# Third and fourth layer norms moved by batches into the experts' loop and the mixer's steps, with the near experts gated and added in one instruction

## The reference, cut to what matters

```
x = x + attention(norm(x))     # 16 heads, top-32 scores of each row, three mixing rounds
x = x + experts(norm(x))       # route each token to one of 8 experts, capacity T/8
x = x + mixer(norm(x))         # conv, chunked state space scan, inner norm, projection
x = x + experts(norm(x))       # the same experts again

norm(x)    = (x - mean) / sqrt(var + 1e-5)
experts(x): logits = x @ wg; one expert a token, a position in it by a running count;
            y = gate * (x @ W[expert].T + b[expert]), gate 0 where the expert is full
mixer(u):   z, xBC, dt = u @ W_in.T; dt = softplus(dt + bias); ...
```

## Time and profile before

| | us |
|---|---|
| median of three runs (lowest, highest) | 2993.7 (2985.3, 3005.35) |
| the profiled execution, as timed | 2987.16 |
| its span in the profile | 2985.5 |
| busy in the span: DVE, PE | 2681.5 (90%), 2536.5 (85%) |
| busy in the span: POOL, ACT | 2258.9 (76%), 2064.4 (69%) |

### The profile page before, as it was taken

How to read it: one execution, slowest core, us unless ns; L and a number is a source line. 1 busy time by engine, 2 the same in 40 slices (tenths; PEclk the granted TensorE clock), 3 DMA queues, 4 the chain that set the end, 5 groups by cost and what they waited for, 6 DMA issues and landing times. The chain is left out here.

```text
span 2985.5 us, 56906 instructions
## 1 busy us (share of the span) xinstructions
PE 2536.5 (85%) x16480; PEld 1487.4 (50%) x16480; DVE 2681.5 (90%) x6598; ACT 2064.4 (69%) x6275; POOL 2258.9 (76%) x2816
## 2 busy tenths in 40 slices
PE   5788888888888888888888888888888787998857
PEld 3444444444444444444444444454444435777733
DVE  7999999999999999999999999999999374766646
ACT  3788888888888888888888888888887242222214
POOL 4899999999999999998998999999989251222105
PEclk7899999999999999999999999999999796767769
DMA  4444444444444444444444444444443000000001
GB/s 122 119 123 118 120 117 121 124 119 124 119 119 117 121 121 120 121 121 120 117 120 117 122 120 124 120 124 118 123 114 106 12 23 15 8 8 0 1 12 47
DMA packets 373454, 286.18 MB, mean 96 GB/s; under 512 B 30174, under 2 KB 369192, under 8 KB 373160
## 3 DMA queue, kind: packets, MB, share of 16 engines
q1 hardware_dynamic: 372232, 280.62, 33.1%
q10 hardware_dynamic: 928, 2.10, 0.2%
HBM read 139.48 MB, written 136.58 MB: 92 GB/s over the span
## 5 line engine op out<-in xcount | busy, mean ns | idle before, releaser
L1038 DVE MAX8 top<-work 128x8 f32<-128x512 f32 x1536 | 1012.5, 723 | 0.0
L1047 DVE MATCH_REPLACE8 work<-top,work 128x512 f32<-128x512 f32 x1024 | 707.1, 720 | 0.0
L1124 POOL TENSOR_TENSOR scores<-scores,cut 128x512 f32<-128x512 f32 x512 | 642.1, 1276 | 0.0
L657 PE MATMUL bank<-probs_t,u 128*64 128x512 f32 x2048 | 475.0, 606 | 11.5 <-ACT u L893 1.4
L1116 POOL TENSOR_SCALAR cut<-scores,minus_max_and_least 128x512 f32<-128x512 f32 x512 | 355.8, 695 | 46.9
L945 ACT ACTIVATE probs_of_tile<-scores,minus_max_and_least 128x512 f32<-128x512 f32 x512 | 376.3, 767 | 14.6 <-POOL scores L1124 14.6
L1137 POOL TENSOR_SCALAR probs_of_tile<-probs_of_tile,inverse 128x512 f32<-128x512 f32 x512 | 350.8, 696 | 26.9 <-DVE inverse L1004 1.4
L1047 DVE MATCH_REPLACE8 work<-top,scores 128x512 f32<-128x512 f32 x512 | 353.2, 719 | 0.0
L1035 DVE MAX8 top<-scores 128x8 f32<-128x512 f32 x512 | 336.5, 721 | 7.8 <-ACT scores L886 6.7
L1120 POOL TENSOR_SCALAR cut<-cut 128x512 f32<-128x512 f32 x512 | 306.6, 615 | 21.6
L864 ACT ACTIVATE band<-band 128x129 f32<-128x129 f32 x512 | 155.2, 305 | 225.6 <-DMA band<-probs_scratch 225.3
(11 more groups left out here) (272 smaller groups left out, 5080.5 us busy)
## 6 DMA issues: line engine op xcount, KB each, us to landing
probs_scratch<-probs_of_tile SPq DMA_DIRECT2D x256, 256.0 KB, 2.4
band<-probs_scratch SPq DMA_DIRECT2D x256, 256.0 KB, 3.2
rel_scratch<-rel SPq DMA_DIRECT2D x256, 254.0 KB, 3.1
relj<-rel_scratch SPq DMA_DIRECT2D x256, 128.0 KB, 2.3
relj<-rel_scratch SPq DMA_DIRECT2D x512, 64.0 KB, 2.5
experts_xs<-stream_normed_t SPq DMA_DIRECT2D x16, 256.0 KB, 2.3
stream<-in_L_attn_a_x SPq DMA_DIRECT2D x4, 512.0 KB, 8.4
mixer_xs<-stream_normed_t SPq DMA_DIRECT2D x8, 256.0 KB, 2.4
```

The costliest lines, as they stand in the source:

```text
L657: last = nc.tensor.matmul(U[HEADS[h], lo:hi], lhs, pt[mpar][:, h, jt, lo:hi], start=(jt == 0 and lo == 0), stop=(jt == NT - 1 and step > 0))
L1038: nc.vector.max(top[q][:, h, 8 * rnd:8 * rnd + 8], work[:, h, :]).then_inc(s.next_tops, 1)
L1047: nc.vector.match_replace(out=work[:, h, :], in_to_replace=top[q][:, h, 8 * rnd:8 * rnd + 8], in_values=sc[Tc][:, h, :] if rnd == 0 else w ...
L1124: nc.gpsimd.tensor_tensor(sc[Tc][:, h, :], sc[Tc][:, h, :], cut[:, h, :], ALU.add).then_inc(s.masked, 1)
```

## The change

The two `norm` blocks, their buffers and helpers, and `eight_tensor` are removed. The third norm is done group by group inside the loop of experts1, the fourth inside the mixer's steps:

- DVE: `group_merge`, four `bn_stats` and four `bn_aggr`, once POOL has added a group into the stream (experts1, after tile 2 of the next group) or after the batch's last `into_stream` (mixer).
- POOL: `group_shift`, two small instructions (variance + eps, minus the mean), the power, and one product that gives the shift.
- ACT: `group_spread`, four `Identity` activations with scale and bias per row, in place of the DVE scaling. It stands at the end of ACT's work on the following group (experts1) or of the step (mixer).
- PE: `group_turn` (four transposes), ACT: `group_keep` (the copy to `XNT`), PE: `group_products` (four tiles of 8 columns). In experts1 the transposes of group i-2 come behind the gate transposes of group i. In the mixer they go into bank `PX` ahead of the projections, which from batch 3 on wait for ACT's copy; the products go into the spare columns of `T1` at the end of the step, ACT copies them out, and from batch 3 on the next step's first write to `T1` waits for that copy (`logits_kept`). The mixer gets one step more.

In both experts, the loads `xs` and `gs` are gone: PE reads `XNT` and the gates in place. The buffer `near` is gone: for each tile DVE issues four `scalar_tensor_tensor` (near bank times gate, plus far) that write `sums`, after ACT's far gating; the near bank is now free only after them. The gate transposes and the bias have one bank each instead of two. All loops over groups and steps are written out instead of run by a loop. The output goes out in eight DMAs of 256 KB, each once its group is done. Last, at the start of the attention, POOL's eight additions of the output bias wait until DVE has scaled all groups, where each waited for its own.

```diff
+def group_merge(nc, dve, s, w, X, i):
+    for c in range(4):
+        last = nc.vector.bn_stats(w.stats[:, i, c, :], X[:, (i * 4 + c) * D:(i * 4 + c + 1) * D])
+    last.then_inc(s.stats, 1)
+    dve.wait_ge(s.stats, i + 1)
+    for c in range(4):
+        last = nc.vector.bn_aggr(w.mv[:, i, c, :], w.stats[:, i, c, :])
+    last.then_inc(s.merged, 1)
+
+def group_shift(nc, pool, s, w, i):
+    pool.wait_ge(s.merged, i + 1)
+    nc.gpsimd.tensor_scalar(w.vareps[:, i, :], w.mv[:, i, :, 1], EPS, 1.0, ALU.add, ALU.mult).then_inc(s.parts, 1)
+    nc.gpsimd.tensor_scalar(w.minus[:, i, :], w.mv[:, i, :, 0], -1.0, 0.0, ALU.mult, ALU.add).then_inc(s.parts, 1)
+    pool.wait_ge(s.parts, 2 * i + 2)
+    nc.gpsimd.tensor_tensor(w.rstd[:, i, :], w.vareps[:, i, :], w.mhalf[:, :], ALU.pow).then_inc(s.rstd, 1)
+    pool.wait_ge(s.rstd, i + 1)
+    nc.gpsimd.tensor_tensor(w.shift[:, i, :], w.minus[:, i, :], w.rstd[:, i, :], ALU.mult).then_inc(s.shift, 1)
+
+def group_spread(nc, act, s, w, X, i, xn):
+    act.wait_ge(s.shift, i + 1)
+    for c in range(4):
+        last = nc.scalar.activation(xn[:, c * D:(c + 1) * D], X[:, (i * 4 + c) * D:(i * 4 + c + 1) * D], ACT.Identity,
+                                    scale=w.rstd[:, i, c:c + 1], bias=w.shift[:, i, c:c + 1])
+    last.then_inc(s.scaled, 1)
...
             for b in range(B):
-                pool.wait_ge(first.scaled, b + 1)
+                pool.wait_ge(first.scaled, GROUPS)
```

In the experts' loop, on PE:

```diff
+                if follow and i >= 2:
+                    late(i - 2)
                 for c in range(4):
...
-                            pe.wait_ge((near_scaled, far_scaled)[q], i * 4 + c - 1)
-                        nc.tensor.matmul(bank[:, :], xs[par][:, c * P:(c + 1) * P],
+                            pe.wait_ge((summed, far_scaled)[q], t - 1)
+                        nc.tensor.matmul(ps[2 * (c % 2) + q][:, :], k.XNT[:, t * P:(t + 1) * P],
...
+                    if c == 2 and follow and i >= 2:
+                        group_products(nc, pe, follow, i - 2, follow.W, k.XNT, EIGHT)
```

On ACT:

```diff
+                    if c == 0 and follow and i >= 2:
+                        group_keep(nc, act, follow, i - 2, TURN, k.XNT)
+                if follow and i:
+                    group_spread(nc, act, follow, gw, k.X, i - 1, gw.xn[:, (i - 1) % 2, :])
```

On DVE (`stats(i)` waits for `stream_added` of group i and calls `group_merge`):

```diff
+                    dve.wait_ge(far_scaled, t + 1)
+                    for e in range(4):
+                        cols = slice(e * P, (e + 1) * P)
+                        last = nc.vector.scalar_tensor_tensor(
+                            out=sums[par][:, c, cols], in0=ps[2 * (c % 2)][:, cols],
+                            scalar=b.gate8[:, t * E + e:t * E + e + 1], in1=far[c % 2][:, cols],
+                            op0=ALU.mult, op1=ALU.add)
...
+                    if c == 2 and follow and i:
+                        stats(i - 1)
```

In the mixer's steps, on PE (`first_half`, `projections`, and the body of a step):

```diff
                 if c == 0:
                     pe.wait_ge(m.silu, j * 3 + 3)
+                    if j >= 3:
+                        pe.wait_ge(m.logits_kept, j - 2)
...
+                if j >= 3:
+                    pe.wait_ge(follow.kept, j - 2)
                 nc.tensor.matmul(PX[:, :], r.win[:, P:2 * P], xs[par][:, :],
...
+                if (done := i - 2) >= 0:
+                    if cur is not None:
+                        pe.wait_ge(m.conv_in, cur * 3 + 1)
+                    group_turn(nc, pe, follow, done, gw.xn[:, done % 2, :], PX, k.ident, 1)
                 if front is not None:
                     projections(front, 1 - par, pairs)
...
+                if done >= 0:
+                    pe.wait_ge(follow.kept, done + 1)
+                    if cur is not None:
+                        pe.wait_ge(m.turned_used, (cur + 1) * NT)
+                    for c in range(NT):
+                        t = done * NT + c
+                        last = nc.tensor.matmul(T1[:, 3 * P + c * E:3 * P + (c + 1) * E], k.XNT[:, t * P:(t + 1) * P],
+                                                follow.W, start=True, stop=True)
+                    last.then_inc(follow.products, 1)
```

On ACT, at the end of a step:

```diff
+                if back is not None:
+                    group_spread(nc, act, follow, gw, k.X, back, gw.xn[:, back % 2, :])
+                if done >= 0:
+                    act.wait_ge(follow.products, done + 1)
+                    nc.scalar.activation(follow.logits[:, done * NT * E:(done + 1) * NT * E],
+                                         T1[:, 3 * P:3 * P + NT * E], ACT.Copy).then_inc(m.logits_kept, 1)
```

More of the change, by code:

```diff
@@ L1356, in _, with late @@
         @block.tensor
         def _(pe):
-            def body(i, par, first, half=0):
-                pe.wait_ge(gs_in[par], (half + 1) * 16)
-                if not first:
-                    pe.wait_ge(g_kept, i - 1)
+            def late(i):
+                group_turn(nc, pe, follow, i, gw.xn[:, i % 2, :], TURN, k.ident, 1)
+            for i in range(GROUPS):
+                par = i % 2
+                if i:
+                    pe.wait_ge(g_kept, i)
                 for c in range(4):
-                    last = nc.tensor.transpose(ps[4 + par][0:E, c * P:(c + 1) * P], gs[par][:, c * E:(c + 1) * E],
-                                               k.ident[:, :])
+                    at = (i * 4 + c) * E
+                    last = nc.tensor.transpose(GT[0:E, c * P:(c + 1) * P], b.gate8[:, at:at + E], k.ident[:, :])
@@ L1783, in body @@
                     nc.gpsimd.tensor_tensor(w.rstd[:, :], w.vareps[:, :], w.mhalf[:, :], ALU.pow).then_inc(m.rstd, 1)
+                if back is not None:
+                    group_shift(nc, pool, follow, gw, back)
             run_steps(pool, body)
@@ L1913, in body @@
                     into_stream(NT - 1)
+                    dve.wait_ge(m.out_added, (back + 1) * NT)
+                    group_merge(nc, dve, follow, gw, k.X, back)
                 if front is not None:
@@ L1984, in program @@
         k.zeros = keep("zeros", [P, 2 * P])
-        w = norm_buffers(keep, "norm")
-        norms = norm_sems(sem, "norm")
         r = Namespace()
@@ L2039, in program @@
         with ExitStack() as ctx:
[L2040 to L2041 removed]
+            norm3.W = r.wdt[:, :]
+            experts(nc, sem, allocate(ctx), ps, k, r, "experts1", norm2, norm3, gw)
         with ExitStack() as ctx:
[L2043 to L2044 removed]
+            norm4.W = r.wg[:, :]
+            norm4.logits = k.logits
+            mixer(nc, sem, allocate(ctx), ps, k, r, norm3, norm4, gw)
         with ExitStack() as ctx:
[L2046 to L2047 removed]
+            experts(nc, sem, allocate(ctx), ps, k, r, "experts2", out=out, logits=k.logits)
 def kernel(**inputs):
```

286 lines of the change are left out of this document (80 added, 206 removed).

## The result

The changed kernel took 3025.5 us (median of 4 runs, 3021.3 to 3033.6), the kernel before 2989.5 beside it (4 runs, 2980.2 to 3005.4): a ratio of 1.013, 95% interval 1.010 to 1.016. Against 0.6% forecast it is slower by 1.3%: inside the range of 2966 to 3052, and just past the 1% by which faster, same and slower were parted, so of my three cases the one with 0.35 came, not the one with 0.53. It is close: a later comparison on another chip gave 1.0097 (1.0069 to 1.0125), which lies on that line. The profiled execution took 3024.3 us, its span is 3022.5, 37.0 over the span before.

What follows compares the result with a forecast made beforehand. DVE bounds the attention, PE the experts1 loop and mixer steps, so what PE waits for matters most. Terms summed to +18.7 us on the 2993.7 median: 3012.4 us, 0.6% slower; range 2966 to 3052.

Steps and rivals of the forecast that it cites:

- the one with 0.35: Whole kernel: the case that it gets slower, over 3023.6 us; chance 0.35.
- the one with 0.53: Whole kernel: the case of no change, within about 1% either way; chance 0.53.
- The attention's start: Attention's start: with POOL waiting, DVE's scaling ends sooner and DVE starts earlier; -3 us, bounds -3.8 and 0.
- The queue in experts1: Experts1, groups 2 to 7: PE idles 4.2 us for the late scaling, plus added work; 5.8 us a group.
- The clock in experts1: Experts1, groups 2 to 7: PE resumes at 1.2 GHz after each stall; 1.8 us a group, bounds 1.3 to 6.1.
- The norms' own stretches: Stretches with only a norm: third falls from 35.6 to 9.0 us (-26.6), fourth ends at -22.9.
- store: Kernel's end: the last eighth of the output takes 2.6 us after its issue instead of 9.1; -6.3.
- The mixer's seams: Between mixer steps: PE waits for ACT's late scaling and copy; 4.9 us at each of six seams, +29.4.
- Experts2: Experts2: near bank held longer, 0.7 us a group, less the load gone; +2.8 us, bounds 0 and +10.
- (b): Experts1: stalls keep the clock at 1.2 GHz through groups 2 to 7; 88.8 instead of 45.6, 3056 us; chance 0.16.
- (c): Both experts: DVE's four instructions take 1.7 us a tile, not 1.11; +19 on top, 3031 us; chance 0.08.
- (a): Experts1 and mixer: scaling done before PE asks, so only PE's added work counts; -39.4, 2954 us; chance 0.14.

Runs made afterwards that it cites:

- b1_wait: Kernel before, with only POOL's bias additions at the attention's start waiting until DVE has scaled all groups; ratio 0.9971, 2979.6 us.
- b2_fused: Kernel before, with only the near experts' gating and adding fused into four DVE instructions a tile, in both experts; ratio 1.0074, 3001.6 us.
- f1_filler: Changed kernel, with four useless 512-column PE products in the experts1 stall of groups 2 to 7; 2987.1 us, ratio 1.0035.
- a_again: Changed kernel run once more, unaltered, beside other runs on another chip; ratio 1.0097, 3014.5 us.
- f4_swap: Changed kernel, with ACT's copy of the logits put ahead of its four scalings at the end of a mixer step; 3016.2 us, ratio 1.0129.
- f3_mixer: Changed kernel, with the norm's scaling, transposes, copy and products moved to the middle of the mixer's step; 2990.1 us, ratio 1.0043.
- f5_both: Changed kernel, with the norm's work reordered in both experts1 and the mixer; 2936.7 us, ratio 0.9859.
- f2_order: Changed kernel, experts1 only: ACT scales after tile 0, PE transposes after tile 2, small products at the group's end; 2960.2 us, ratio 0.9944.

## Why the prediction was right, and where it was off

**The attention's start: right.** -3 with a bound of -3.8; the first search came at 39.45, -4.1, of which 3.85 are the shorter scaling, and b1_wait bears it out. The whole stage ended 7.9 earlier in the two spans, but the ten executions with the changed attention end their first gates anywhere from 2353.5 to 2362.4, and b2_fused, with the old attention, at 2359.9, so the other 4 can't be laid to the change.

**The queue in experts1: right.** Stall 4.2 predicted, 4.12 to 4.22 measured; 5.8 us a group for the queue, 5.77 measured by f1_filler (14.36 less 8.59). The unknown instructions: the four of DVE 1.13 (1.11 taken), POOL's four from 2385.42 to 2387.28 (1.8 taken), ACT's scaling 1.65 (1.5 taken).

**The clock in experts1: mis-sized, the one term that moved the result.** I took 1.8 us a group between bounds of 1.3 and 6.1, "near the lower, since nothing interrupts PE once it resumes". In the profiled execution it was the upper bound, about 6.1 in every group: 6 x (20.45 - 8.59) = 71.2 instead of 45.6. After each stall PE worked without a pause and still ran over 11 us at 1.2 GHz, as it had at the start of experts1; I preferred the 2.6 us seen in experts2. What those rows showed was two outcomes of one event, and not a low figure with an exception. a_again has both. Halfway between my bounds, 3.7 us a group, the sum would have been +30, 1.0% slower; with a_again's mean of 4.5 it would have been +35, 1.2%. The runs gave 1.3% and 1.0%. The rule quoted in the prediction from the Trainium skill, "TensorE: Matmul & The Clock Gate", section HAM oscillation, says that such a loop starts each round throttled. By f1_filler's comparison the trace agrees in direction and goes past the price that I gave it: 37 us in the profiled execution, not 10.8. In a_again the rounds are slow at their start too, but one begins fast and two are cheap. E1 in all grew by 67.2, where I had 45.3: +25.6 by this term, and -3.7 in the rest, most of it because PE came to speed sooner at the start of the stage: its first group took 11.7 us instead of 14.6 (the first bias product starts 4.35 us after PE's first work, as before, but is 1.15 instead of 2.07 long).

**The norms' own stretches: right.** 9.0 predicted, 9.0 measured; 9.6 predicted, 9.7 measured, and the mixer's last step grew by 4.7 where I had 4.3; store -6.3, measured -6.8; load -2.5, as measured.

**The mixer's seams: the sum came, and in part by luck.** 29.4 predicted for six seams; M grew by 26.9 (26.9 to 34.6 in the four executions with this mixer, 45.4 in the fifth, the slow one). Both waits were where the prediction had them, side by side (f4_swap). Their sizes were not. From the third step on PE's first transpose into `T1` starts 6.33 us after the power where it started 2.1 to 2.3 after, 4.1 later, not 3.1: beside DVE's `silu` POOL's four instructions took 2.94 us, not the 1.8 that I had from the attention. The projections start 5.0 to 7.0 later, not 4.2. Against that, the delay did not all stay, as I had it: the six steps grew by 2.2, 7.2, 8.9, 1.5, 7.4 and -0.5 us. The last, which has no projections, met the same wait and took 39.67 us against 40.13. The clock's share is also larger than the 0.7 a seam taken for it. M before, in the changed kernel and in f3_mixer:

```profile
2592.25:2836.75 244.50, 220.53 (x1160) 184.38 (x1159) 166.14 (x467) 66.56 (x131) 51.10 (x28) 0.70 0.01 4
2625.26:2896.65 271.39, 239.35 (x1230) 199.01 (x1230) 157.98 (x515) 79.62 (x166) 64.65 (x52) 0.67 0.01 4
2617.41:2869.15 251.74, 232.05 (x1232) 193.12 (x1231) 164.02 (x515) 79.94 (x167) 65.51 (x53) 0.70 0.01 4
```

Of the 19.7 us that f3_mixer gains on the changed kernel, 12.3 are idle time of PE and 7.3 are busy time for the same work: the clock, 1.2 a seam in this execution. In the five executions with the changed mixer PE is idle 29 to 32 us in M and busy from 239 to 260, so their spread is the clock's as well. That a mean clock of 0.69 is near a point at which it switches, as the prediction says, no run shows. What f3_mixer leaves, 7.2 over before and 1.5 over b2_fused, is too near the spread of equal mixers to be split further.

**Experts2: low.** +2.8 predicted, +6.3 measured, for the near bank held longer is 1.01 us a group (9.60 against 8.59), not 0.7. PE waits at tile 3, as its timeline shows in the changed kernel; two gate transposes stand 9.60 apart:

```profile
2954.57 0.60 PE L1264 MATMUL bank<-identity,experts_gate 128*8 128x128 f32 x4
...
2962.35 1.98 PE L1273 MATMUL bank<-rest_we,stream_normed_t 128*128 128x512 f32 x4 [0.74 <-DVE experts_sums L1335]
2964.17 0.60 PE L1264 MATMUL bank<-identity,experts_gate 128*8 128x128 f32 x4
```

It is within the bound of +10.

**The sum.** 37.0 measured against 18.7: experts1 +21.9, attention -4.9, experts2 +3.5, the seams -2.5, and 0.3 in the rest. That the total is off by only 18 us owes something to luck: the attention's -4.9 can't be told from scatter between executions, and the seams' errors cancel.

**The rivals.** (b), the clock down throughout, came in part: not 23.4 us a group but 20.4, so 71.2 on the six groups against its 88.8, since the clock rose again in each. (c) did not happen. (a) is the one that teaches most. It was worked out as -39.4 for a kernel in which the scaling is done before PE asks; f5_both, which is that kernel, measured -40.1. That the two agree to 1 us is chance, for terms offset each other: M grew by 5.2 where 13.2 was put down, E2 by 10.0 where 2.8 was (3.1 of it a first group of 14.6 us, at 1.2 GHz, against 11.5 in the changed kernel). But the same instructions are in both kernels, and the interval of f5_both is all below 1: what made the change slower was its order.

**Open.** Why the same pause costs 1.7 us once and 6 another time; the profile shows the granted clock, not what sets it. And why f2_order's mixer took 289.9 us where four others with the same code took 271 to 279: PE is idle as long as in them and busy 11 us longer than in the next, so it is the clock, in the slowest of that kernel's executions, and what led to it is not known.

## What to carry to other kernels

When work is folded into a loop, follow the last thing that it waits for back through every queue, and place the consumer at least that far behind; the same instructions made the kernel 1.3% slower in one order and 2.0% faster in another. Price a pause of the tensor engine of some microseconds by its own length and again by slow work behind it, and take both of the outcomes that the trace shows, not the kinder. And look at who holds a PSUM bank before fusing two passes: the fusion cost 22 us by itself, and cost the group's period nothing once the slower producer's product came first.

## What was not expected of the hardware

- **The clock after a pause.** Pauses of 4.1 to 4.2 us at the same place of the same loop were followed by 1.2 GHz for under 5 us or for over 11, with no work missing on PE in either. In a_again after 2404.67 PE even began fast (four transposes in 0.66) and fell only then. Useless products in the pause kept 2.4 GHz in all groups of f1_filler.
- **GpSimd beside VectorE.** The first two instructions of `group_shift` (128x4) took 0.20 us each and the power 1.02 in experts1, where VectorE stood or gated out of PSUM, and 0.54 and 1.44 at the mixer's seam beside VectorE's `silu`. Eight scalings of VectorE took 2.35 us alone and 6.20 beside GpSimd's additions. The Trainium skill says in "GPSIMD Engine Reference", section Key points, that the two share their SBUF interfaces and contend in some forms of VectorE's instructions; the trace agrees, in both directions.
